# Weights laid out on the host so that each partition's row is contiguous: a recurrent attention and slot-memory layer on 8 cores

## The chip, the cores and the metric

The kernel runs as one program on all 8 cores of one Trainium2 chip. Each core owns 2048 of the 16384 token rows and writes that part of the output. Where a sum over the batch element is needed, a core goes through all 8192 rows of its batch element itself; the cores exchange nothing. The metric is the device time of the slowest core, in microseconds (us).

## What is computed

```python
x = L0_attn_q_x                      # (2, 8192, 1024)
xn = _layernorm(x)
s = attn(xn)                         # linear attention (elu + 1 features), wq, wk, wv, wo,
                                     # then an MLP 1024 -> 4096 -> 1024 (fc_w, proj_w)
g = silu(ffn(xn))                    # slot memory, below
return x + s * g

# ffn(x):
S = slot_init                        # 64 slots
ctx = concat(x, mean of S over the slots)
h = gelu(ctx @ w1 + b1)              # w1: (2048, 512)
route_logits = (h @ w2 + b2) / (abs(tau) + 0.1)
alpha = softmax over the top 8 of 64 logits
si = (alpha.T @ x) / alpha.sum(over rows)
S_new = GRU(si, S)                   # Wih, Whh: (3072, 1024)
q, k, v = S_new @ wq, S_new @ wk, S_new @ wv       # wq, wk: (1024, 256)
y = layernorm(S_new + softmax(q @ k.T * scale) @ v)
out = alpha @ (y @ wvp + bvp) @ wo + bo
```

The reference is in f32; the kernel multiplies in bf16 and holds sums in f32.

## The kernel before

`make_core_inputs` prepares each core's inputs on the host, `build_nc` writes the program. All weights come from HBM as f32 and are cast to bf16 on the way into SBUF, by DMAs that GpSimd (POOL) issues. The helper for this is `cast_load` (line 202): a weight of `nchunk` x 128 rows and `width` columns goes to an SBUF tile in which partition p holds row p of every chunk, side by side. Its source access pattern has three dimensions, so per partition it reads `nchunk` separate pieces of `width` f32 numbers:

```python
src = bass.AP(src_t.tensor, src_row0 * width,
              [[width, 128], [width * 128, nchunk], [1, width]])
```

The work is cut into blocks (`with nc.Block()`), and the engines meet in a barrier at the end of each block. Four blocks hold the loads that the change touches:

- Block 1 (line 309): SP issues 14 small loads of constants and then the first eight 512 KB tiles of x (`xld`). POOL issues w1ab (`w1a`, the upper half of w1: 8 chunks of 512 columns), w1bb (4 chunks of the lower half), w2b, slotTb, B2R, and eight tiny writes to `scr_qk`. Behind the barrier follow a few small operations on `tau` and the slot mean, and four matmuls on w1bb (line 379).
- Block 2 (line 390): POOL alone issues the other 4 chunks of w1bb, then wqb, wkb and wvb (8 chunks of 1024 columns each). Behind it come four matmuls on w1bb (line 405), a transpose and an addition, then phase A.
- Phase A (line 506): 16 tiles of 512 rows. For each: layernorm statistics (lines 524, 526), transposes, the multiplication with w1ab, logits, top 8, slot sums. wqb, wkb and wvb aren't used here; they are first read near 957 us.
- Block 3 (line 899): POOL issues a bias row, slotTb, fwqb and fwkb (8 chunks of 256 columns each) and four rows of whhT (1 chunk of 3072 columns each, 12 KB of f32 per partition). Behind it the slot GRU and the slot attention follow, with weights streamed in single chunks (whhT, wihT, fwv, wvp, fwo).
- Block 4 (line 1382): SP loads a mask; POOL issues wob (8 chunks of 1024 columns) and four bias rows. Behind it, attention and its output projection go through the 4 own tiles.

At the end the MLP runs. Its weights already lie on the host as 128 rows of 32768 numbers. fcw is loaded in pieces of 1024 numbers per partition (`load_fc`, line 1838) and pjw in pieces of 4096 (`load_pj`, 16 KB of f32 in one piece), both from rows 128 KB apart.

The DMAs increment semaphores (`swA` for w1, w2, fwq and fwk; `swB` for wq, wk, wv and wo), and `X` keeps the counts that later blocks wait for.

Of the kernel before, what the change touches and what calls it, by code (L numbers as in the profile page):

```python
# [14 lines left out]
D = 1024  # L15
# [6 lines left out]
NS, TOPK = 64, 8  # L22
DHF = 512
# [5 lines left out]
    return np.ascontiguousarray(np.asarray(v, np.float32).reshape(nchunk, 128).T)  # L29


def make_core_inputs(c, inp):
    import ml_dtypes
    BF = ml_dtypes.bfloat16
    g = lambda k: np.asarray(inp["L0_" + k], dtype=np.float32)
    b = c // 4
    r0 = (c % 4) * T_OWN
    x = g("attn_q_x")[b]
    return {
        "x8k": np.ascontiguousarray(np.concatenate([x[r0:], x[:r0]], axis=0)),  # L40
        "wq": g("attn_wq"), "wk": g("attn_wk"), "wv": g("attn_wv"),
        "wo": g("attn_wo"),
        "fcw": np.ascontiguousarray(
            g("attn_fc_w").reshape(8, 128, 4, 8, 128)
            .transpose(1, 2, 3, 0, 4).reshape(128, 32768)),
        "pjw": np.ascontiguousarray(
            g("attn_proj_w").reshape(32, 128, 8, 128)
            .transpose(1, 2, 0, 3).reshape(128, 32768)),
        "w1a": np.ascontiguousarray(g("ffn_w1")[0:D]),
        "w1b": np.ascontiguousarray(g("ffn_w1")[D:]),  # L50
        "w2": g("ffn_w2"),
        "wihT": np.ascontiguousarray(g("ffn_Wih").T),
        "whhT": np.ascontiguousarray(g("ffn_Whh").T),
        "fwq": g("ffn_wq"), "fwk": g("ffn_wk"), "fwv": g("ffn_wv"),
        "wvp": g("ffn_wvp"), "fwo": g("ffn_wo"),
        "slotT": np.ascontiguousarray(g("ffn_slot_init").T),
        "slot": g("ffn_slot_init"),
        "ln1w_c": _cols(g("attn_ln1_w"), 8), "ln1b_c": _cols(g("attn_ln1_b"), 8),
        "ln2w_c": _cols(g("attn_ln2_w"), 8), "ln2b_c": _cols(g("attn_ln2_b"), 8),
        "lng_c": _cols(g("ffn_ln_g"), 8), "lnb_c": _cols(g("ffn_ln_b"), 8),  # L60
        "fcb_c": _cols(g("attn_fc_b"), 32), "pjb_c": _cols(g("attn_proj_b"), 8),
        "b1_c": _cols(g("ffn_b1"), 4),
        "fbq_c": _cols(g("ffn_bq"), 2), "fbk_c": _cols(g("ffn_bk"), 2),
        "b2r": g("ffn_b2")[None, :],
        "bq_r": g("attn_bq")[None, :], "bk_r": g("attn_bk")[None, :],
        "bv_r": g("attn_bv")[None, :], "bo_r": g("attn_bo")[None, :],
        "bih_r": g("ffn_bih")[None, :], "bhh_r": g("ffn_bhh")[None, :],
        "fbv_r": g("ffn_bv")[None, :], "bvp_r": g("ffn_bvp")[None, :],
        "fbo_r": g("ffn_bo")[None, :],
        "tau": g("ffn_tau").reshape(1, 1),  # L70
        "identb": np.eye(128, dtype=np.float32).astype(BF),
        "identf": np.eye(128, dtype=np.float32),
        "mask4": np.ascontiguousarray(np.tile(
            (np.arange(128)[:, None] // 16 ==
             np.arange(128)[None, :] // 16).astype(np.float32), (1, 4))),
        "onesb": np.ones((1, 512), np.float32).astype(BF),
        "onecol": np.ones((128, 1), np.float32).astype(BF),
        "magic": np.full((128, 1), 0x5f3759df, np.int32),
        "zpad": np.zeros((1024, 64), dtype=BF),
    }  # L80


def build_nc(dbg=False):
    nc = bass.Bass("TRN2", target_bir_lowering=False)

    di = lambda n, s, dt=F32: nc.dram_tensor(n, s, dt, kind="ExternalInput").ap()
    x8k = di("x8k", [T_B, D])
    wq_d = di("wq", [D, D]); wk_d = di("wk", [D, D]); wv_d = di("wv", [D, D])
    wo_d = di("wo", [D, D])
    fcw_d = di("fcw", [128, 32768]); pjw_d = di("pjw", [128, 32768])  # L90
    w1a_d = di("w1a", [D, DHF]); w1b_d = di("w1b", [D, DHF]); w2_d = di("w2", [DHF, NS])
    wihT_d = di("wihT", [D, 3 * D]); whhT_d = di("whhT", [D, 3 * D])
    fwq_d = di("fwq", [D, 256]); fwk_d = di("fwk", [D, 256]); fwv_d = di("fwv", [D, D])
    wvp_d = di("wvp", [D, D]); fwo_d = di("fwo", [D, D])
    slot_d = di("slot", [NS, D]); slotT_d = di("slotT", [D, NS])
    ln1w_d = di("ln1w_c", [128, 8]); ln1b_d = di("ln1b_c", [128, 8])
# [39 lines left out]
    with ExitStack() as ex:  # L136
# [65 lines left out]
        def cast_load(g, dst2d, src_t, nchunk, width, dst_off=0, src_row0=0,  # L202
# [9 lines left out]
            else:  # L212
                C['wt'] += 16

        def chunked(t2d, nchunk, width):
            return t2d[:, 0:nchunk * width].rearrange("p (c w) -> p c w",
                                                      c=nchunk)
# [48 lines left out]
        with ExitStack() as exW:  # L266
# [6 lines left out]
            with ExitStack() as exA:  # L273
# [35 lines left out]
                with nc.Block() as blk:  # L309
                    @blk.sync  # L310
                    def _(s):
                        for src, dst in [(identb_d, cIDb[:]),
                                         (onesb_d, cONE[:]), (onecol_d, cCOL[:]),
                                         (magic_d, cMAG[:]),
                                         (b1_d, B1E[:]),
                                         (ln1w_d, LNC[:, 0:8]), (ln1b_d, LNC[:, 8:16]),
                                         (ln2w_d, LNC[:, 16:24]), (ln2b_d, LNC[:, 24:32]),
                                         (lng_d, LNC[:, 32:40]), (lnb_d, LNC[:, 40:48]),
                                         (fcb_d, BC[:, 0:32]), (pjb_d, BC[:, 32:40]),
                                         (fbq_d, FBC[:, 0:2]), (fbk_d, FBC[:, 2:4]),  # L320
                                         (tau_d, SCAL[0:1, 0:1])]:
                            dma(s, dst, src[:], sld, 'ld')
                        for st in range(4):
                            dmx(s, xslot(0, st), x8k[st * 128:(st + 1) * 128, :],
                                sx[0], 'x0')
                        for st in range(4):
                            r = 512 + st * 128
                            dmx(s, xslot(1, st), x8k[r:r + 128, :], sx[1], 'x1')

                    @blk.gpsimd  # L330
                    def _(g):
                        g.memset(SCAL[:, 7:8], EPS)
                        cast_load(g, w1ab, w1a_d, 8, DHF, sem=swA, key='wA')
                        cast_load(g, w1bb, w1b_d, 4, DHF, sem=swA, key='wA')
                        cast_load(g, w2b, w2_d, 4, NS, sem=swA, key='wA')
                        cast_load(g, slotTb, slotT_d, 8, NS, sem=swA, key='wA')
                        dmx(g, B2R[:], b2r_d[:], swA, 'wA')
                        for mt4 in range(4):
                            for half in range(2):
                                po = (mt4 * 8194 + half * 4097 + 4096) * 128  # L340
                                dmx(g, bass.AP(scr_qk, po, [[1, 128]]),
                                    bass.AP(zpad_d.tensor, 0, [[1, 128]]),
                                    swB, 'wB')
# [46 lines left out]
                with nc.Block() as blk:  # L390
                    @blk.gpsimd
                    def _(g):
                        cast_load(g, w1bb, w1b_d, 4, DHF, src_row0=512,
                                  sem=swA, key='wA')
                        cast_load(g, wqb, wq_d, 8, D, sem=swB, key='wB')
                        cast_load(g, wkb, wk_d, 8, D, sem=swB, key='wB')
                        cast_load(g, wvb, wv_d, 8, D, sem=swB, key='wB')

                with nc.Block() as blk:
                    @blk.tensor  # L400
# [466 lines left out]
            with ExitStack() as exB3:  # L867
# [31 lines left out]
                with nc.Block() as blk:  # L899
                    @blk.sync  # L900
                    def _(s):
                        dma(s, slotb[:], slot_d[:], sld, 'ld')

                    @blk.gpsimd
                    def _(g):
                        dmx(g, ROWB3[0:1, 0:3072], bhh_rd[:], swA, 'wA')
                        cast_load(g, slotTb2, slotT_d, 8, NS, sem=swA, key='wA')
                        cast_load(g, fwqb, fwq_d, 8, 256, sem=swA, key='wA')
                        cast_load(g, fwkb, fwk_d, 8, 256, sem=swA, key='wA')
                        for c0 in range(4):  # L910
                            cast_load(g, wslot(c0), whhT_d, 1, 3072,
                                      src_row0=c0 * 128,
                                      sem=swc4[c0], key=wk4[c0])
# [444 lines left out]
            with ExitStack() as exC:  # L1358
# [23 lines left out]
                with nc.Block() as blk:  # L1382
# [3 lines left out]

                    @blk.gpsimd
                    def _(g):
                        cast_load(g, wob, wo_d, 8, D, sem=swB, key='wB')
                        for srcd, i2 in [(bq_rd, 0), (bk_rd, 1), (bv_rd, 2),  # L1390
                                         (bo_rd, 3)]:
                            dmx(g, rowA(i2), srcd[:], swB, 'wB')
# [733 lines left out]
```

How the kernel before makes its waits and increments, by code:

```python
                    @blk.vector  # L348
                    def _(v):
                        v.wait_ge(sld, ld_p0)
                        v.wait_ge(swA, X['wA'])
                        t0 = SCAL[0:1, 0:1]
                        v.tensor_scalar(SCAL[0:1, 1:2], t0, -1.0, None, ALU.mult)
# [18 lines left out]
                    @blk.tensor  # L372
                    def _(t):
                        t.wait_ge(sdv, C['dv'])
                        t.matmul(pM0[:, 0:1], cONE[0:1, 0:128], SCB[0:1, 0:1],
                                 start=True, stop=True)
                        i = None
                        for cc in range(4):
                            i = t.matmul(pM1[0:1, 0:512], smT[:, cc:cc + 1],
                                         w1bb[:, cc * 512:(cc + 1) * 512],
                                         start=(cc == 0), stop=False)
                        fin(i, spe, 'pe')
# [1 line left out]
                    @blk.vector  # L384
                    def _(v):
                        v.wait_ge(spe, C['pe'])
                        i = v.tensor_copy(SCAL[:, 5:6], pM0[:, 0:1])
                        finv(v, sdv, 'dv')
# [11 lines left out]
                    @blk.tensor  # L400
                    def _(t):
                        t.wait_ge(swA, X['wA'])
                        i = None
                        for cc in range(4):
                            i = t.matmul(pM1[0:1, 0:512], smT[:, 4 + cc:5 + cc],
# [1441 lines left out]
                @blk.gpsimd  # L1847
                def _(g):
                    g.wait_ge(sy1, X['y1'])
                    for q in range(4):
```

## Time and profile before

| | us |
|---|---|
| median of 2 runs | 2354.45 (2351.16 to 2357.73) |
| profiled execution | 2343.93 |
| its span, slowest core (core 2) | 2342.4 |
| its span, fastest core (core 3) | 2321.8 |

| engine | busy us | share of the span |
|---|---|---|
| TensorE, matmul | 1206.5 | 52% |
| VectorE | 534.1 | 23% |
| ScalarE | 502.8 | 21% |
| GpSimd | 74.7 | 3% |

The profile is of core 2, the slowest. Times within it count from the first instruction of the core in question, so times of two cores are comparable only as far as the cores start together. "GB/s" in a row is what the DMA engines wrote: a weight that is read as f32 and written as bf16 counts with its bf16 bytes, and twice as many were read. The DMA share is the mean busy share of the core's 16 DMA engines; it goes over 1 where packets overlap. A packet is one contiguous piece of a DMA. The letter q behind an engine's name stands for its instruction queue: SPq and POOLq rows are DMA issues and waits, not work.

### The profile page before, as it was taken

Reading aid. Unit: us, or ns where it says so; the run is one execution under the profiler, and the core shown is the slowest. Engines: PE = TensorE matmul, PEld = TensorE weight load, DVE = VectorE, ACT = ScalarE, POOL = GpSimd, SP = SyncE. Lnnn points to the kernel's source line nnn. Section 1 sums busy time; section 2 is a strip of 40 time slices with the busy share of each in tenths; the row PEclk is TensorE's granted clock in tenths of the full one; section 3 lists DMA queues with packets and bytes.
Section 4 is the critical chain, followed back from the end, with each engine's and each line's share of the span. In section 5 each row is a group of like instructions: output and inputs, shape, how many; then the busy total and the mean of one; then the engine's idle time right before and its main releaser. Section 6 shows DMA issues by size and latency. Waiting matters only on the chain. (4 is left out here: it accounts for less than half of the span.)

```text
span 2342.4 us, 18749 instructions; the slowest of 8 cores (2321.8 to 2342.4 us)
## 1 busy us (share of the span) xinstructions
PE 1206.5 (52%) x6220; PEld 568.2 (24%) x6308; DVE 534.1 (23%) x1213; ACT 502.8 (21%) x748; POOL 74.7 (3%) x139
## 2 busy tenths in 40 slices
PE   0143535444533322644734825823078598598696
PEld 0021222222211100222321312311034243243242
DVE  0223133233210110323233233221210310400102
ACT  0144443443420100100100200200041330431521
POOL 1000000000000011000000000001100000000000
PEclk9976667777767555767867957957589799799798
DMA  7511011111046435152332331345903605506224
GB/s 133 107 52 72 36 72 37 71 72 71 2 59 120 73 51 85 50 104 63 86 68 63 86 77 54 99 77 119 196 14 72 180 1 101 151 11 120 85 39 105
DMA packets 185777, 183.65 MB, mean 78 GB/s; under 512 B 141331, under 2 KB 145556, under 8 KB 181588
## 3 DMA queue, kind: packets, MB, share of 16 engines
q0 software_dynamic: 26496, 72.72, 18.3%
q1 hardware_dynamic: 159188, 109.74, 16.3%
q8 instruction: 53, 0.87, 0.2%
q14 instruction: 40, 0.33, 0.0%
HBM read 204.81 MB, written 33.56 MB: 102 GB/s over the span
## 5 line engine op out<-in xcount | busy, mean ns | idle before, releaser
L690 PE MATMUL pM<-xnTs,w1ab 128*128 128x512 bf16 x496 | 141.9, 451 | 52.4 <-ACTq L199 52.0
L676 PE MATMUL pT<-cIDb,xnb 128*128 128x128 bf16 x256 | 31.6, 301 | 243.7 <-ACTq L199 156.2
L1948 DVE TENSOR_TENSOR y1t<-pTf,y1t 128x512 f32<-128x512 f32 x32 | 22.1, 692 | 503.0 <-PE pTf L2042 503.0
L2011 PE MATMUL pMa<-h2T,fcwb 128*128 128x512 bf16 x496 | 125.5, 393 | 21.2 <-ACTq L199 20.5
L2011 PE MATMUL pMb<-h2T,fcwb 128*128 128x512 bf16 x504 | 122.7, 386 | 0.4
L2028 PE MATMUL pPa<-g1F,pjcb 128*128 128x512 bf16 x500 | 111.8, 379 | 5.4 <-ACTq L199 4.5
L1611 ACT ACT_TABLE_LOAD x4 | 5.1, 1283 | 505.9 <-PE pBig L1564 505.9
L2028 PE MATMUL pPb<-g1F,pjcb 128*128 128x512 bf16 x504 | 112.7, 379 | 0.9 <-DMA pjcb<-pjw 0.2
L524 DVE BATCH_NORM_STATS2 ST<-xld 128x6 f32<-128x512 f32 x64 | 43.6, 681 | 281.6 <-ACTq L199 281.1
L1995 PE MATMUL pT0d<-cIDb,h2b 128*128 128x128 bf16 x128 | 16.3, 307 | 145.0 <-DVEq L199 84.5
L690 PEld LDWEIGHTS pM<-xnTs,w1ab 128*128 128x128 bf16 x512 | 56.0, 113 | 134.6 <-issue 99.5
L1440 PE MATMUL pBig<-wob,aoT 128*128 128x512 bf16 x248 | 71.0, 450 | 29.8 <-DVEq L199 29.8
L676 PEld LDWEIGHTS pT<-cIDb,xnb 128*128 128x128 bf16 x256 | 24.1, 135 | 250.6 <-issue 250.6
L1556 PE MATMUL pBig<-wqb,xhT 128*128 128x512 bf16 x252 | 64.3, 413 | 17.0 <-ACTq L199 16.1
L1777 DVE TENSOR_TENSOR AMK<-pBig,cMSK 128x512 bf16<-128x512 f32 x64 | 44.3, 692 | 121.6 <-PE pBig L1733 91.8
L2011 PEld LDWEIGHTS pMa<-h2T,fcwb 128*128 128x128 bf16 x512 | 50.9, 100 | 83.7 <-issue 27.7
L1733 PE MATMUL pBig<-FQ2h,FK2h 64*128 64x128 bf16 x256 | 31.2, 296 | 75.7 <-DMA scr_ao<-aog 69.5
L2011 PEld LDWEIGHTS pMb<-h2T,fcwb 128*128 128x128 bf16 x512 | 51.0, 100 | 63.8 <-issue 6.1
L2028 PEld LDWEIGHTS pPa<-g1F,pjcb 128*128 128x128 bf16 x512 | 49.6, 98 | 63.7 <-issue 6.8
L2070 ACT ACTIVATE h2T<-pT0d,LNC 128x128 bf16<-128x128 bf16 x128 | 58.5, 457 | 27.2 <-PE pT0d L1995 15.3
L2028 PEld LDWEIGHTS pPb<-g1F,pjcb 128*128 128x128 bf16 x512 | 49.8, 98 | 58.1 <-issue 1.3
L1752 PE MATMUL pBig<-V2h,AMK 128*128 128x64 bf16 x256 | 24.7, 214 | 73.1 <-DVEq L199 73.1
(263 smaller groups left out, 1721.0 us busy)
## 6 DMA issues: line engine op xcount, KB each, us to landing
xld<-x8k SPq DMA_DIRECT2D x64, 512.0 KB, 5.3
pjcb<-pjw POOLq DMA_DIRECT2D x32, 1024.0 KB, 8.7
scr_qk<-tmb SPq DMA_DIRECT2D x16, 512.0 KB, 2.6
y1scr<-XN SPq DMA_DIRECT2D x4, 2048.0 KB, 6.6
y1t<-y1scr SPq DMA_DIRECT2D x4, 2048.0 KB, 11.5
fcwb<-fcw POOLq DMA_DIRECT2D x32, 256.0 KB, 17.3
xre<-x8k SPq DMA_DIRECT2D x16, 512.0 KB, 10.1
out<-xre SPq DMA_DIRECT2D x16, 512.0 KB, 2.7
```

The costliest lines, as they stand in the source:

```text
L524: v.bn_stats(ST[:, SB[st]:SB[st] + 6], xslot(mt, st)[:, 0:512])
L676: i = t.transpose(dstb[:, cc * 128:(cc + 1) * 128], xb[:, cc * 128:(cc + 1) * 128], cIDb[:])
L690: i = t.matmul(dstp[:, 0:512], w1ab[:, cc * 512 + ch * 128: cc * 512 + (ch + 1) * 128], xnTs[:, cc * 512:(cc + 1) * 512], start=(cc == 0), ...
L1440: i = t.matmul(pBig0[:, nh * 512:(nh + 1) * 512], aoT[:, cc * 128:(cc + 1) * 128], wob[:, cc * 1024 + nh * 512: cc * 1024 + (nh + 1) * 512 ...
L1556: i = t.matmul(pBig0[:, nh * 512:(nh + 1) * 512], xhT[:, cc * 512 + st * 128: cc * 512 + (st + 1) * 128], wqb[:, cc * 1024 + nh * 512: cc ...
L1733: i = t.matmul(pBig0[:, (b % 2) * 512 + gl * 128: (b % 2) * 512 + (gl + 1) * 128], FK2h[0:64, g * 128:(g + 1) * 128], FQ2h[0:64, g * 128:( ...
L1752: t.matmul(pBig1[:, (B2 % 2) * 512 + gl * 64: (B2 % 2) * 512 + (gl + 1) * 64], amsl, V2h[:, g * 64:(g + 1) * 64], start=True, stop=True)
L1777: i = v.tensor_tensor(AMK[:, (b % 2) * 512:(b % 2 + 1) * 512], pBig0[:, (b % 2) * 512:(b % 2 + 1) * 512], cMSK[:], ALU.mult)
L1948: i = v.tensor_tensor(y1v(mt).rearrange("p (s w) -> p s w", s=4)[:, :, d * 128:(d + 1) * 128], pTf[:, :].rearrange("p (s w) -> p s w", s=4 ...
L2011: i = t.matmul(dstp[:, :], fcwb[:, m * 1024 + cc * 128: m * 1024 + (cc + 1) * 128], h2T[:, cc * 512:(cc + 1) * 512], start=(cc == 0), stop ...
L2028: i = t.matmul(dstp[:, :], pjcb[:, (d % 2) * 4096 + m * 128: (d % 2) * 4096 + (m + 1) * 128], g1F[:, m * 512:(m + 1) * 512], start=(m == 0 ...
L2070: i = a.activation(h2T[:, cc * 512 + st * 128: cc * 512 + (st + 1) * 128], pT0d[:, cc * 128:(cc + 1) * 128], AF.Identity, bias=LNC[:, 24 + ...
```

## The change

The host now stores eight weights (wq, wk, wv, wo, both halves of w1, and the slot attention's wq and wk) the way they will lie in SBUF: 128 rows, in row p the pieces of all chunks for partition p. A second helper, `cast_loadh`, reads them with two dimensions, one contiguous run per partition, into the same tile on the same semaphore. The lower half of w1 is loaded in two parts as before, columns 0 to 2047 and 2048 to 4095 of its row. Order, engines, semaphores and all other loads stay. w2, slotT, fwv, wvp, fwo, wihT and whhT keep their layout and `cast_load`.

```diff
+def _rm128(a):
+    n = a.shape[0] // 128
+    return np.ascontiguousarray(
+        a.reshape(n, 128, -1).transpose(1, 0, 2).reshape(128, -1))
...
-        "wq": g("attn_wq"), "wk": g("attn_wk"), "wv": g("attn_wv"),
-        "wo": g("attn_wo"),
+        "wq": _rm128(g("attn_wq")), "wk": _rm128(g("attn_wk")),
+        "wv": _rm128(g("attn_wv")),
+        "wo": _rm128(g("attn_wo")),
...
-        "w1a": np.ascontiguousarray(g("ffn_w1")[0:D]),
-        "w1b": np.ascontiguousarray(g("ffn_w1")[D:]),
+        "w1a": _rm128(g("ffn_w1")[0:D]),
+        "w1b": _rm128(g("ffn_w1")[D:]),
...
-        "fwq": g("ffn_wq"), "fwk": g("ffn_wk"), "fwv": g("ffn_wv"),
+        "fwq": _rm128(g("ffn_wq")), "fwk": _rm128(g("ffn_wk")),
+        "fwv": g("ffn_wv"),
...
+        def cast_loadh(g, dst2d, src_t, nchunk, width, col0=0, tot=None,
+                       sem=None, key=None):
+            tot = nchunk * width if tot is None else tot
+            src = bass.AP(src_t.tensor, col0, [[tot, 128], [1, nchunk * width]])
+            g.dma_start(out=dst2d[:, 0:nchunk * width],
+                        in_=src).then_inc(sem, 16)
+            X[key] += 16
...
-                        cast_load(g, w1ab, w1a_d, 8, DHF, sem=swA, key='wA')
-                        cast_load(g, w1bb, w1b_d, 4, DHF, sem=swA, key='wA')
+                        cast_loadh(g, w1ab, w1a_d, 8, DHF, sem=swA, key='wA')
+                        cast_loadh(g, w1bb, w1b_d, 4, DHF, tot=4096,
+                                   sem=swA, key='wA')
...
-                        cast_load(g, w1bb, w1b_d, 4, DHF, src_row0=512,
-                                  sem=swA, key='wA')
-                        cast_load(g, wqb, wq_d, 8, D, sem=swB, key='wB')
-                        cast_load(g, wkb, wk_d, 8, D, sem=swB, key='wB')
-                        cast_load(g, wvb, wv_d, 8, D, sem=swB, key='wB')
+                        cast_loadh(g, w1bb, w1b_d, 4, DHF, col0=2048,
+                                   tot=4096, sem=swA, key='wA')
+                        cast_loadh(g, wqb, wq_d, 8, D, sem=swB, key='wB')
+                        cast_loadh(g, wkb, wk_d, 8, D, sem=swB, key='wB')
+                        cast_loadh(g, wvb, wv_d, 8, D, sem=swB, key='wB')
...
-                        cast_load(g, fwqb, fwq_d, 8, 256, sem=swA, key='wA')
-                        cast_load(g, fwkb, fwk_d, 8, 256, sem=swA, key='wA')
+                        cast_loadh(g, fwqb, fwq_d, 8, 256, sem=swA, key='wA')
+                        cast_loadh(g, fwkb, fwk_d, 8, 256, sem=swA, key='wA')
...
-                        cast_load(g, wob, wo_d, 8, D, sem=swB, key='wB')
+                        cast_loadh(g, wob, wo_d, 8, D, sem=swB, key='wB')
```

## Rows read from the trace of the kernel before

**Rows 1.** The page: its head, and the queue of POOL's DMAs.

```profile
span 2342.4 us, 18749 instructions; the slowest of 8 cores (2321.8 to 2342.4 us)
...
q0 software_dynamic: 26496, 72.72, 18.3%
```

**Rows 2.** Operations at the four lines (ns min/median/max, first and last start us).

```profile
L309 POOLq DRAIN  x1: 30830/30830/30830, 6.9 to 6.9; - x1
...
L390 POOLq DRAIN  x1: 44234/44234/44234, 45.0 to 45.0; - x1
...
L899 POOLq DRAIN  x1: 27932/27932/27932, 682.6 to 682.6; - x1
...
L1382 POOLq DRAIN  x1: 13783/13783/13783, 923.7 to 923.7; - x1
```

**Rows 3.** Timeline, 0 to 140 us: start us, us, instruction.

```profile
1.60 1.04 POOL L208 DMA_DIRECT2D w1ab<-w1a  x1 [0.44 <-issue]
...
14.07 100.35 SPq L191 DMA_DIRECT2D xld<-x8k  x12
...
43.68 0.81 POOL L208 DMA_DIRECT2D w1bb<-w1b  x1 [34.29 <-PEq L390]
...
89.65 1.86 PE L405 MATMUL pM<-w1bb,smT 128*1 128x512 bf16 x4 [47.08 <-PEq L390]
```

**Rows 4.** DMA: an issue (KB, median us to landing); all packets of 40 to 95 us.

```profile
B2R<-b2r POOLq DMA_DIRECT2D x1, 0.1 KB, 30.1
...
DMA packets 3648, 6.82 MB, mean 124 GB/s; under 512 B 64, under 2 KB 576, under 8 KB 3648
```

**Rows 5.** Stretches, core 2: busy us by engine, PEclk, DMA share, GB/s.

```profile
4.00:8.00 4.00, 0.00 (x0) 0.00 (x0) 0.00 (x0) 0.00 (x0) 4.00 (x9) 1.00 0.95 92
8.00:14.00 6.00, 0.00 (x0) 0.00 (x0) 0.00 (x0) 0.00 (x0) 1.39 (x3) 1.00 1.12 136
46.00:47.00 1.00, 0.00 (x0) 0.00 (x0) 0.00 (x0) 0.00 (x0) 1.00 (x2) 1.00 0.04 3
48.00:88.00 40.00, 0.00 (x0) 0.00 (x0) 0.00 (x0) 0.00 (x0) 0.00 (x0) 1.00 1.07 168
684.00:692.00 8.00, 0.00 (x0) 0.00 (x0) 0.00 (x0) 0.00 (x0) 0.92 (x2) 0.50 1.18 148
692.00:700.00 8.00, 0.00 (x0) 0.00 (x0) 0.00 (x0) 0.00 (x0) 0.00 (x0) 0.50 1.02 159
700.00:704.00 4.00, 0.00 (x0) 0.00 (x0) 0.00 (x0) 0.00 (x0) 0.00 (x0) 0.50 1.02 209
924.00:932.00 8.00, 0.00 (x0) 0.00 (x0) 0.00 (x0) 0.00 (x0) 0.85 (x2) 0.50 1.08 193
1642.00:1654.00 12.00, 0.00 (x0) 0.00 (x0) 0.00 (x0) 0.00 (x0) 3.09 (x7) 0.50 1.07 158
1837.00:1839.00 2.00, 2.00 (x11) 0.89 (x10) 0.00 (x0) 0.00 (x0) 0.00 (x0) 1.00 1.11 233
1845.00:1849.00 4.00, 2.12 (x4) 0.39 (x4) 2.45 (x2) 2.16 (x5) 0.00 (x0) 0.61 1.04 178
2306.00:2307.00 1.00, 0.03 (x1) 0.06 (x1) 0.00 (x0) 0.69 (x1) 0.53 (x1) 1.00 0.00 0
```

**Rows 6.** The same view for core 3.

```profile
692.00:700.00 8.00, 0.00 (x0) 0.00 (x0) 0.00 (x0) 0.00 (x0) 0.00 (x0) 0.50 0.95 146
700.00:704.00 4.00, 1.82 (x5) 0.85 (x6) 0.00 (x0) 0.00 (x0) 0.00 (x0) 0.50 0.01 2
```

**Rows 7.** The same view: first core 0, then core 1.

```profile
43.00:48.00 5.00, 0.00 (x0) 0.00 (x0) 0.00 (x0) 0.00 (x0) 0.00 (x0) 1.00 1.15 206
...
43.00:46.00 3.00, 0.00 (x0) 0.00 (x0) 0.00 (x0) 0.00 (x0) 3.00 (x4) 1.00 0.05 4
```

**Rows 8.** Timeline of POOL: two DMA issues.

```profile
922.01 0.91 POOL L208 DMA_DIRECT2D wob<-wo  x1 [9.13 <-PEq L1382]
...
2306.39 0.53 POOL L1868 DMA_DIRECT2D pjcb<-pjw  x1 [8.12 <-PE pPb L2028]
```

More of the change, by code:

```diff
@@ L87, in build_nc @@
     x8k = di("x8k", [T_B, D])
-    wq_d = di("wq", [D, D]); wk_d = di("wk", [D, D]); wv_d = di("wv", [D, D])
-    wo_d = di("wo", [D, D])
+    wq_d = di("wq", [128, 8192]); wk_d = di("wk", [128, 8192])
+    wv_d = di("wv", [128, 8192]); wo_d = di("wo", [128, 8192])
     fcw_d = di("fcw", [128, 32768]); pjw_d = di("pjw", [128, 32768])
-    w1a_d = di("w1a", [D, DHF]); w1b_d = di("w1b", [D, DHF]); w2_d = di("w2", [DHF, NS])
+    w1a_d = di("w1a", [128, 4096]); w1b_d = di("w1b", [128, 4096])
+    w2_d = di("w2", [DHF, NS])
     wihT_d = di("wihT", [D, 3 * D]); whhT_d = di("whhT", [D, 3 * D])
-    fwq_d = di("fwq", [D, 256]); fwk_d = di("fwk", [D, 256]); fwv_d = di("fwv", [D, D])
+    fwq_d = di("fwq", [128, 2048]); fwk_d = di("fwk", [128, 2048])
+    fwv_d = di("fwv", [D, D])
     wvp_d = di("wvp", [D, D]); fwo_d = di("fwo", [D, D])
```

## The prediction

> **What bounds the kernel now.** I read first the page's head and its DMA queues. The span is 2342.4 us on the slowest core and 2321.8 us on the fastest, and the queue of POOL's DMAs, the one that all the edited loads use, is busy for only 18.3% of it [rows 1]. So most of the span (TensorE, ScalarE and VectorE working in a chain) can't be touched by a layout of weights. Next I read the operations recorded at the lines of the four blocks in which the edited loads stand. Each of these blocks ends in a barrier, and before it POOL runs a DRAIN that lasts until POOL's own DMAs have landed: 30.8, 44.2, 27.9 and 13.8 us, 116.7 us together [rows 2]. I call the blocks 1 to 4. No compute engine works in that time. The timeline shows it: the first of the four loads of block 2, w1bb, is issued at 43.68, and the matmul at line 405, which needs nothing but this w1bb (0.52 MB, first in the queue), starts at 89.65 [rows 3]. What the barrier waits for is the last, wvb, which the kernel first multiplies much later. So a microsecond taken from one of these four drains is a microsecond of the span, and this holds for nothing else in the change.
>
> The question is therefore what sets the speed of these loads: the number of pieces, or the bytes. In the stretch of block 2 the trace counts 3648 packets for 6.82 MB [rows 4]. That is one per row piece of 4 KB f32 (3 x 1024, 2 KB when written as bf16) or 2 KB f32 (512), and 64 small ones. The rate is 168 GB/s written, so 336 GB/s read, at a DMA share of 1.07: the engines always have something to do [rows 5].
>
> **The pairs.** In block 3 whhT arrives in rows of 12 KB f32, 6 KB written, three times larger than the pieces of wq. Core 2 gets 159 GB/s there from 692 to 700 us. At 700 core 3 falls from 146 to 2 GB/s, and core 2 rises to 209 [rows 5, 6]. So two neighbouring cores share something, and what a core gets depends on the other one. Held against this, the small pieces do as well: core 0 loads its second w1bb and the beginning of wq (1 KB and 2 KB written) at 206 GB/s between 43 and 48 us, while core 1 moves 4 GB/s [rows 7]. With the neighbour at work, pieces of 2 KB get 168 (wq, wk, wv) and 158 (fcw, rows 128 KB apart), pieces of 6 KB 159 and pieces of 8 KB (pjw) 178. Alone, 2 KB gets 193 to 206, 6 KB 209, 8 KB 233 [rows 5, 7]. Under load, which is how all cores stand in blocks 1 and 2, there is no gain in the size of the piece.
>
> **The change part by part.** It touches w1 (1.57 MB written in block 1, 0.52 MB in block 2), wq, wk and wv (6.29 MB, block 2), fwq and fwk (1.05 MB, block 3) and wo (2.10 MB, block 4), 11.54 MB in all. Bytes, order, semaphores, barriers and what lands where in SBUF stay as they are. Each load becomes 128 rows instead of 512 or 1024 pieces, so the queue's 26496 packets [rows 1] fall by 896 (w1a), 2 x 384 (w1b), 4 x 896 and 2 x 896, to 19456. The edited loads now take about 11.6 us (1.57 MB at 136 GB/s, block 1), 40.6 us (6.82 at 168), 7.1 us (1.05 at 148) and 10.9 us (2.10 at 193) [rows 5], together 70 us.
>
> Block 2. First the start. w1bb is issued at 43.68 and its data flows from about 47.0 (3 GB/s in the microsecond before) [rows 3, 5]: 3.3 us for 512 pieces, with 3072 more behind them. A load of 128 pieces, pjcb at 2306.39, moves data from 2307 on (0 GB/s before) [rows 5, 8]: 0.6 us. The difference, 2.7 us, is the upper bound. The lower is 0, for part of those 3.3 us may be paid by any first DMA after a barrier. I take 2.0, nearer to the pjcb row. Then the rate: 168 stays, 0 us. The lower bound is the slowest loaded row, 158, which costs 6.82/0.158 - 40.6 = +2.6 us. The upper is 209, worth -8.0 us. I take the row of pieces three and four times larger under load (159, 178), which brackets what is there.
>
> The Trainium skill has a price for a small packet (DMA: Bandwidth & Descriptors, "Why small descriptors are slow"): about 3 cycles on top of one per 32 bytes. As an estimate from that page, this would make 1 KB pieces 9% and 2 KB pieces 4 to 5% faster once they are long, some 4.5 us over all edited loads, and a result near 2344. The 206 GB/s of pieces of 1 and 2 KB beside 209 of 6 KB don't show it.
>
> Block 1. w1ab is issued at 1.60 and 92 GB/s flow between 4 and 8 us; from 8 to 14 us, before x is asked for, it is 136 [rows 3, 5]. At the 168 of block 2 the 1.57 MB would take 9.4 us instead of 11.6: 2.2 us, and data after 0.6 instead of 2.4 us adds up to 1.8. But what the drain waits for is not w1: the tiny B2R, issued before the drain begins at 6.9 us, needs 30.1 us to land [rows 2, 4], while the eight x loads (4.2 MB, issued by SP from 14.07 us [rows 3]) run on the same engines until the drain ends at 37.7. What the weights free must first be used by x. Bounds 0 and 4.0; I take 2.0.
>
> Block 3. slotT stays in 1024 small pieces in front. fwq and fwk, with the smallest pieces of all edited loads (512 bytes written), come between 684 and 692 us, at 148 GB/s [rows 5]: 7.1 us. At 168 they would take 6.2, so 0.9 us is the gain in rate, and up to 1 more if POOL's making of 2048 descriptors holds up whhT behind them; nothing at least. I take 1.0.
>
> Block 4. wob is issued at 922.01 and the drain ends at 923.7 + 13.8 = 937.5 [rows 2, 8]: 15.5 us, of which 10.9 are data at 193 GB/s. The rest is the start, four bias rows and the end. The start can give back 2.7 us at most, as in block 2, and nothing at least; a mask load of SP fills part of it, so I take 1.0.
>
> The rest costs nothing: POOL's issues get shorter, but POOL goes straight into its drain. The weights are used long after, so no later wait changes, and a stall doesn't move to another place: the barrier is released by the same DMA a little earlier. Should w1 become faster than x in block 1, x is late next, and that is the 0 of its bound.
>
> **Sum.** 2.0 + 2.0 + 1.0 + 1.0 = 6.0 us. The profiled execution took 2343.9 us (span 2342.4 and 1.5 around it), so it would be 2337.9. The median shown is 2354.45, 10.5 above it, and its two runs lie 6.6 us apart. From the median I come to 2354.45 - 6.0 = 2348.
>
> **The rivals.** A, the layout doesn't bring larger packets: if the rows are cut again into the old pieces, all stays, 2354.5. For it: each row of 32 KB f32 is longer than any piece of before (16 KB f32, pjw). Against: the pieces that the code asks of POOL with pjw's uncut (24064), and 16 small packets for each of its 134 DMAs as in block 2 (64 for 4), come to 26208, close to the 26496 counted [rows 1, 4].
>
> B, the pieces do set the rate under load. Then what is shared by a pair would serve long rows better, and all edited bytes come at 209 GB/s: 11.54/0.209 = 55 instead of 70 us, and with 4 us of starts the gain is 19: 2335. For it: 8 KB alone does best (233). Against: 159 and 178 under load, beside 168 for the pieces of now.
>
> C, the long rows are slower. Pieces that were neighbours in one 512 KB stretch of HBM become 128 streams whose starts lie 32 KB apart (16 KB for w1, 8 KB for fwq), and such streams may hit the same part of the memory. If all edited loads fell to the poorest rate of a busy stretch, 92 GB/s (4 to 8 us) [rows 5], they would take 11.54/0.092 = 125 us, 55 more: 2409, slower by 2.3%. It decides against the change once the edited loads together take more than the 4 us that the starts give back, at a mean of 11.54/74 = 156 GB/s against 11.54/70 = 165 now, and it passes 2% (47 us) at 99 GB/s. Against it: fcw and pjw already have rows 128 KB apart and get 158 and 178 under load [rows 5]. The Trainium skill has such a rule (DMA: Bandwidth & Descriptors, "Latency and other measured facts"): row pitches of large powers of two slow a copy, halving it at 4 MiB. The pitches here are far below those it lists, and no run here shows it.
>
> **How the numbers follow.** The small gain of the sum 0.62, A 0.16, B 0.10, C in a mild form (up to +20 us) 0.08, C in full 0.04. The range runs from under B's 2335 to a mild C or a poor run, 2328 to 2362; the two runs of before alone span 2351 to 2358. Faster by over 2% (about what a measurement of this kernel can tell from no change, 47 us) would need 40% of all four drains: 0.01. Slower by over 2% is C in full: 0.04. Within 2%: 0.95.
>
> **What the profile after would show.** The queue of POOL at about 19456 packets; 576 packets for 6.82 MB in block 2; issues of the edited loads at the 0.53 us of pjcb [rows 8] instead of 0.9; the DRAIN of line 390 ending near 85 us instead of 45.0 + 44.2 = 89.2 [rows 2] (2.0 from block 1 and 2.0 of its own; its start moves with the shorter issues, so its end is what counts), and the one of 1382 about a microsecond shorter; the rate of block 2 near 168. If that rate is 200 or more, B is right and I have taken a limit of pieces for one of the pair. If it is under 150, C is. If all this holds and the time still moves by more than 10 us, the cause lies outside these blocks, for instance in the rhythm of the long phases (the cores of before already differ by 20 us [rows 1]), and my sum was of the wrong thing.

## The result, and the profile after

| | before | after |
|---|---|---|
| median, us | 2351.85 (10 runs) | 2335.68 (12 runs) |
| ratio, after to before | | 0.9922, 95% interval 0.9901 to 0.9943 |
| profiled execution, us | 2343.93 | 2330.59 |
| span, slowest core | 2342.4 | 2329.0 |
| span, mean of the 8 cores | 2333.1 | 2320.4 |

The change takes 0.8%, some 16 to 18 us, where 6 had been forecast: inside the range, faster, and nearly three times the gain. The mean span fell by 12.7 us, the profiled execution by 13.3. The ratios, unlike the medians, leave out every execution in which one half of the cores ran at a lower granted clock, and where the profiled execution was such a one (w1 of block 1 alone, below), its drains are means over the other four cores.

First the page of the changed kernel, its head and the queue of POOL's DMAs (packets, MB, share of the 16 engines). Behind it, all packets of the stretch from 40 to 95 us on core 2 of a kernel described below ("all but that"), whose block 2 has the changed loads and nothing beside them:

```profile
span 2329.0 us, 18837 instructions; the slowest of 8 cores (2307.1 to 2329.0 us)
...
q0 software_dynamic: 19456, 72.72, 18.6%
```

```profile
DMA packets 576, 6.82 MB, mean 124 GB/s; under 512 B 64, under 2 KB 64, under 8 KB 192
```

The packets are those foretold, 19456 and 576, so the rows arrive whole, and rival A is out. The engines' share of the queue, though, is 18.6% against 18.3% [rows 1] for the same bytes (core 2 in both kernels: 18.1 and 18.3): with a quarter fewer packets the DMA engines are busy for about as long.

The four drains of the slowest core, core 7 (operations at the four lines: ns min/median/max, first and last start us), which answer to [rows 2]:

```profile
L327 POOLq DRAIN  x1: 17590/17590/17590, 6.9 to 6.9; - x1
...
L409 POOLq DRAIN  x1: 44918/44918/44918, 31.7 to 31.7; - x1
...
L918 POOLq DRAIN  x1: 28779/28779/28779, 668.5 to 668.5; - x1
...
L1401 POOLq DRAIN  x1: 15102/15102/15102, 909.4 to 909.4; - x1
```

The slowest core isn't the same in both profiles, and cores differ, so the comparison goes by the mean of all eight:

| mean over the cores, us | block 1 | block 2 | block 3 | block 4 | sum |
|---|---|---|---|---|---|
| drain, before | 30.2 | 42.6 | 28.3 | 14.1 | 115.2 |
| drain, after | 16.7 | 44.3 | 27.6 | 12.7 | 101.4 |
| end of the drain, before | 37.1 | 86.9 | 706.6 | 931.6 | |
| end of the drain, after | 23.6 | 75.2 | 695.1 | 920.7 | |

Nearly everything comes from block 1: 13.5 us, of which block 2 takes 1.8 back. The 11 to 12 us that are left after block 2 stay, but for a fraction: 10.9 at the end of block 4's drain.

The same core in both kernels shows where it happens. DMA issues of core 2 up to 39 us (KB, us from issue to landing), first before, then after:

```profile
w1ab<-w1a POOLq DMA_DIRECT2D x1, 1024.0 KB, 13.3
...
slotTb<-slotT POOLq DMA_DIRECT2D x1, 128.0 KB, 18.1
```

```profile
w1ab<-w1a POOLq DMA_DIRECT2D x1, 1024.0 KB, 10.2
...
slotTb<-slotT POOLq DMA_DIRECT2D x1, 128.0 KB, 12.8
...
B2R<-b2r POOLq DMA_DIRECT2D x1, 0.1 KB, 13.2
```

w1ab, the largest load whose layout changed here, lands only 3.1 us sooner. slotTb, which didn't change, gains 5.3 us, and the 128 bytes of B2R gain 17: 13.2 instead of 30.1 [rows 4]. Most of the gain is at loads that the change doesn't touch.

Stretches of the changed kernel on core 2 (columns as in [rows 5]):

```profile
4.00:8.00 4.00, 0.00 (x0) 0.00 (x0) 0.00 (x0) 0.00 (x0) 4.00 (x9) 1.00 0.98 166
8.00:14.00 6.00, 0.00 (x0) 0.00 (x0) 0.00 (x0) 0.00 (x0) 0.81 (x2) 1.00 1.10 152
...
24.00:32.00 8.00, 1.26 (x3) 0.13 (x1) 0.16 (x1) 0.00 (x0) 2.19 (x4) 1.00 1.03 319
...
48.00:72.00 24.00, 0.00 (x0) 0.00 (x0) 0.00 (x0) 0.00 (x0) 0.00 (x0) 1.00 1.00 170
```

At the start w1 flows faster (166 and 152 GB/s against 92 and 136). From 48 to 72 us, when wq, wk and wv come in their long rows, it is 170 against 168 [rows 5]: nothing. And between 24 and 32 us x still flows (319 GB/s, nearly all of it x), while the drain of block 1 has been over since 20.4 us and the first matmuls run. POOL's drain no longer lasts as long as x does.

### The profile page after: what moved, and what is told of

Read it like the earlier page. It is cut to its first block and busy times, and to the rows that moved or that the text cites. A ratio compares the mean times of both kernels' runs of the same rounds, so it can differ in the third digit from the quotient of the medians.

```text
span 2329.0 us, 18837 instructions; the slowest of 8 cores (2307.1 to 2329.0 us)
## 1 busy us (share of the span) xinstructions
PE 1215.7 (52%) x6308; PEld 567.2 (24%) x6308; DVE 533.7 (23%) x1213; ACT 503.0 (22%) x748; POOL 71.8 (3%) x139
## 3 DMA queue, kind: packets, MB, share of 16 engines
q0 software_dynamic: 19456, 72.72, 18.6%
q1 hardware_dynamic: 159188, 109.74, 16.7%
## 5 line engine op out<-in xcount | busy, mean ns | idle before, releaser
L709 PE MATMUL pM<-xnTs,w1ab 128*128 128x512 bf16 x512 | 149.2, 459 | 44.5 <-ACTq L209 44.2
L543 DVE BATCH_NORM_STATS2 ST<-xld 128x6 f32<-128x512 f32 x64 | 43.6, 681 | 280.6 <-ACTq L209 280.0
L2030 PEld LDWEIGHTS pMa<-h2T,fcwb 128*128 128x128 bf16 x512 | 50.8, 100 | 84.3 <-issue 28.3
L2089 ACT ACTIVATE h2T<-pT0d,LNC 128x128 bf16<-128x128 bf16 x128 | 58.6, 458 | 27.3 <-PE pT0d L2014 15.3
```

The lines of the kernel that those rows point to most:

```text
L543: v.bn_stats(ST[:, SB[st]:SB[st] + 6], xslot(mt, st)[:, 0:512])
L709: i = t.matmul(dstp[:, 0:512], w1ab[:, cc * 512 + ch * 128: cc * 512 + (ch + 1) * 128], xnTs[:, cc * 512:(cc + 1) * 512], start=(cc == 0), ...
L2030: i = t.matmul(dstp[:, :], fcwb[:, m * 1024 + cc * 128: m * 1024 + (cc + 1) * 128], h2T[:, cc * 512:(cc + 1) * 512], start=(cc == 0), stop ...
L2089: i = a.activation(h2T[:, cc * 512 + st * 128: cc * 512 + (st + 1) * 128], pT0d[:, cc * 128:(cc + 1) * 128], AF.Identity, bias=LNC[:, 24 + ...
```

## The experiments

The drains are means over the cores of one profiled execution each, in us. Ratios are to the kernel before on the same chip, with 95% intervals. Not all kernels ran on the same chip, so they are compared with each other through their ratios.

| kernel | block 1 | block 2 | block 3 | block 4 | ratio |
|---|---|---|---|---|---|
| before | 30.2 | 42.6 | 28.3 | 14.1 | |
| after | 16.7 | 44.3 | 27.6 | 12.7 | 0.9922 (0.9901 to 0.9943) |
| w1 of block 1 alone (cores 4 to 7) | 17.0 | 45.7 | 29.7 | 14.9 | 0.9956 (0.9939 to 0.9973) |
| all but that | 28.7 | 42.7 | 27.2 | 12.8 | 0.9973 (0.9947 to 1.0000) |
| before, x held back | 15.6 | 46.6 | 29.7 | 15.9 | 0.9978 (0.9958 to 0.9999) |
| after, x held back | 14.0 | 46.4 | 28.6 | 12.4 | 0.9945 (0.9925 to 0.9965) |
| after, x first | 26.5 | 43.6 | 28.4 | 12.9 | one execution, no ratio |
| before, small loads first | 31.1 | 43.8 | 29.3 | 15.2 | 1.0016 (0.9982 to 1.0051) |
| after, w2 and slotT in rows too | 15.3 | 44.1 | 27.3 | 12.6 | 0.9924 (0.9895 to 0.9954) |
| after, wq, wk, wv at the start of phase A | 16.2 | 9.8 | 28.3 | 12.6 | 0.9792 (0.9756 to 0.9829) |
| the last two together | 15.5 | 8.5 | 26.2 | 13.0 | 0.9811 (0.9767 to 0.9855) |
| after, wq, wk, wv spread over phase A | 15.5 | 9.6 | 28.8 | 13.4 | 0.9776 (0.9736 to 0.9815) |
| before, wq, wk, wv spread over phase A | 30.4 | 6.3 | 29.6 | 15.1 | 0.9856 (0.9823 to 0.9888) |

The drain of block 1 before is 31.4 us over cores 4 to 7 alone, 30.2 over all eight.

**The change in two parts.** First block 1's loads of w1 alone:

```diff
-                        cast_load(g, w1ab, w1a_d, 8, DHF, sem=swA, key='wA')
-                        cast_load(g, w1bb, w1b_d, 4, DHF, sem=swA, key='wA')
+                        cast_loadh(g, w1ab, w1a_d, 8, DHF, sem=swA, key='wA')
+                        cast_loadh(g, w1bb, w1c_d, 4, DHF, sem=swA, key='wA')
```

> The kernel before, with only the two loads of w1 in block 1 changed (one contiguous row per partition). Turns theory: each DMA engine takes packets by turns from POOL's queue and SP's, so the small packets behind w1 in POOL's queue (w2b, slotTb, B2R) wait for the x packets of SP once those flow; w1 in fewer packets lets them out before. Then this edit alone shortens the drain of block 1 from a mean of 30.2 us over the cores to about 17 (16.7 in the changed kernel), and gives 11 to 14 of the 16 us: about 2339. Rate theory (long rows are served faster everywhere, my rival B): the gain goes with the bytes, 1.57 of 11.54 MB, so about 2 to 3 us here: about 2349.

Then everything but these two loads:

> The changed kernel, with the two loads of w1 in block 1 put back to pieces: wq, wk, wv, wo, fwq, fwk and the second part of w1b stay contiguous. Turns theory: the drain of block 1 stays at 30 us; block 2 gains its start of 1 to 2 us, block 3 0 to 1, block 4 1.4, in all 3 to 5 us: about 2348. Rate theory: 12 to 14 of the 16 us: about 2338, and the drain of block 2 falls from 42.6 to 36 or less.

w1 alone makes the drain short, 31.4 to 17.0 us as expected, and gives 0.44%, 10 us, a little less than the 11 to 14 expected. All the rest, 9.97 of 11.54 MB, gives 0.27%, 6 us, and leaves block 1 at 28.7. Together that is 0.71% of the 0.78. The intervals of the two ratios overlap (6 to 14 us and 0 to 12), so the times alone don't say which part gives more. But 14% of the bytes bring 10 us, where rival B, by bytes, leaves them 2 to 3, and the drains show where the gain is. So rival B falls although the time of 2335 was its own. The second kernel also gives the clean price of the layout in block 2, since no x runs beside it there, as in the kernel before. Core 2, drain and stretch:

```profile
L409 POOLq DRAIN  x1: 42721/42721/42721, 43.3 to 43.3; - x1
...
48.00:84.00 36.00, 0.00 (x0) 0.00 (x0) 0.00 (x0) 0.00 (x0) 0.00 (x0) 1.00 1.00 162
```

162 GB/s in rows of 16 KB written, 168 in pieces of 2 KB [rows 5], and a mean drain of 42.7 against 42.6 us. A load under way with the neighbour working gains nothing from longer pieces here. The drains of blocks 3 and 4 got 1.1 and 1.3 us shorter. Over all rows of the table block 4's drain is 14.1 to 15.9 us with the old layout of wo and 12.4 to 13.4 with the new, so that about 2 us there are real; in block 3 the two groups overlap (28.3 to 29.7, and 26.2 to 28.8).

**x held back.** SP waits until w1ab, w1bb, w2b, slotTb and B2R have landed (5 x 16) before it asks for x; in the first kernel no layout is changed:

```diff
+                        s.wait_ge(swA, 80)
                         for st in range(4):
                             dmx(s, xslot(0, st), x8k[st * 128:(st + 1) * 128, :],
                                 sx[0], 'x0')
```

> The kernel before, layout untouched; SP asks for x only when w1ab, w1bb, w2b, slotTb and B2R have landed. Turns theory: without x packets to take turns with, the drain of block 1 falls from 30.2 to about 15 us (w1bb landed at 17.7 us, and slotTb and B2R follow in 3 to 5 us), with no layout changed; x then loads beside block 2, whose drain grows by up to 8 us, so the time falls by 5 to 12 us: 2340 to 2347. Descriptor theory (POOL's making of 3584 descriptors holds B2R up, whatever SP does): the drain stays at 26 us or more, and as x comes later the time doesn't fall.

> The changed kernel with the same wait of SP before x. Turns theory: the drain of block 1 is 9 to 13 us on all cores alike (it was 13.5 to 23.1 without the wait), and against the run of the kernel before with this wait the layout is worth only 2 to 4 us in this drain. Time 2332 to 2338, about as the changed kernel. Descriptor theory: a difference of 12 us or more between the two kernels with the wait, as without it.

The drain of block 1 on core 2, in pieces with x held back:

```profile
L309 POOLq DRAIN  x1: 15819/15819/15819, 6.9 to 6.9; - x1
```

Half of the 30.8 us of before [rows 2] are gone with the old layout, and on all cores alike (14.9 to 16.2, where it was 26.1 to 34.8). So the number of pieces in itself, or POOL's making of their descriptors, doesn't hold this drain up: x does. The layout is worth 1.6 us of drain once x is out of the way (15.6 to 14.0); 2 to 4 had been expected, and 9 to 13 us for the drain of 14.0. The time moves less than the drain: 0.9978, 5 us, at the edge of the 5 to 12 expected. x comes later, and in block 2 the drain grows by 4.0 us because x now runs beside it. In the changed kernel the wait gives nothing (0.9945 and 0.9922, the intervals overlap). Block 2 also begins later after the drain, for SP is still issuing x: its drain ends at 78.9, 8.0 us sooner than before. In the kernel in pieces even that is gone by the end of block 4's drain (931.0 against 931.6), with phase A, block 3 and block 4 a little longer each; why is not settled.

**x first.** The changed kernel, with SP's eight x loads ahead of its small ones (the list in the code has 16 of these, not the 14 named ahead of the prediction):

> The changed kernel with the eight x loads issued by SP ahead of its 14 small loads, so that x flows from the start instead of from 11 to 15 us on. Turns theory: now the small packets of POOL's queue (96 per DMA engine for w2b and slotTb) meet the 64 x packets per engine in spite of the contiguous w1, and the drain of block 1 grows from a mean of 16.7 back to 24 us or more, where x ends. If the layout of w1 in itself made the drain short, it stays near 17.

The drain of block 1 and two of the landings on core 2:

```profile
L327 POOLq DRAIN  x1: 26513/26513/26513, 6.9 to 6.9; - x1
...
w1ab<-w1a POOLq DMA_DIRECT2D x1, 1024.0 KB, 14.4
...
slotTb<-slotT POOLq DMA_DIRECT2D x1, 128.0 KB, 25.2
```

With contiguous w1 the drain is long again, 26.5 us in the mean, once x flows from the start. w1ab, first in POOL's queue with 8 large packets per DMA engine, has landed 14.4 us after its issue. slotTb, an eighth of its bytes in 64 small packets per engine, takes 25.2; it stands behind w1ab, w1bb and w2b in the same queue, so this time isn't the price of its own packets alone. What happens in between is seen in the packets of the two queues, q1 of SP (x and the constants) and q0 of POOL (packets, MB, share of 16 engines), on core 2, first from 20 to 26 us, then from 26 to 30:

```profile
q1 hardware_dynamic: 515, 1.79, 86.5%
q0 software_dynamic: 516, 0.06, 16.3%
...
q1 hardware_dynamic: 1914, 0.30, 80.0%
q0 software_dynamic: 1299, 0.13, 53.3%
```

Beside x, POOL's queue gets 516 packets of 128 bytes out in 6 us, one for one of SP's, although it moves a thirtieth of the bytes. From 26 us on, as x runs out (its last packet is through at 28.4), 1299 go in 4 us. The other seven cores show the same, 488 to 559 packets of POOL's beside 495 to 560 of SP's from 20 to 26 us.

**Small loads first.** The kernel before, only POOL's order in block 1 changed; w1ab and w1bb come last:

```diff
-                        cast_load(g, w1ab, w1a_d, 8, DHF, sem=swA, key='wA')
-                        cast_load(g, w1bb, w1b_d, 4, DHF, sem=swA, key='wA')
                         cast_load(g, w2b, w2_d, 4, NS, sem=swA, key='wA')
...
                                     swB, 'wB')
+                        cast_load(g, w1ab, w1a_d, 8, DHF, sem=swA, key='wA')
+                        cast_load(g, w1bb, w1b_d, 4, DHF, sem=swA, key='wA')
```

> The kernel before with only the order of POOL's issues in block 1 changed: w2b, slotTb, B2R and the writes to scr_qk ahead of w1ab and w1bb; the layout stays in pieces, the packet counts too. Turns theory: the 96 tiny packets per engine go out before x flows and 96 packets of 1 KB meet x instead; the drain ends once those have had their turns, somewhere between 17 and 25 us long instead of 30.2, and the time falls by 3 to 10 us. If the number of packets in POOL's queue against the 64 of x per engine is all that counts, the order changes nothing: 28 us or more, as half of the 1 KB packets are still there at 14 us.

```profile
w1ab<-w1a POOLq DMA_DIRECT2D x1, 1024.0 KB, 25.3
...
slotTb<-slotT POOLq DMA_DIRECT2D x1, 128.0 KB, 3.5
```

My 17 to 25 us were wrong, the other figure held: 31.1 us. slotTb now lands after 3.5 us instead of 18.1, but w1ab, in 64 pieces per engine, needs 25.3 instead of 13.3 in the old order. The order chooses the victim, and here too the queues go one for one: 815 packets each on core 2 from 20 to 34 us, POOL's of 1 KB, SP's mostly of 4 KB. The order moved more than I had reckoned with. w1ab is issued at 7.75 us instead of 1.60, behind the eight writes to `scr_qk`, and SP, through with its small loads earlier, asks for x at 8.30 instead of 14.07. So nearly all of w1 met x, where I had expected half of it to be out. Whether an order that gets part of w1 out first would gain anything, no run shows. What decides is how many packets POOL's queue still has when x begins, and they can be pieces of w1 as well as of slotT.

**Fewer pieces still.** w2 and slotT stored in rows as well:

> The changed kernel with w2 and slotT stored as contiguous rows as well (256 packets in place of 1536 in block 1, 128 in place of 1024 in block 3). Turns theory: w2b and slotTb need 8 packets per engine instead of 32 and 64, everything of POOL's is through before x packets matter, and the drain of block 1 falls from a mean of 16.7 to 11 to 13 us on all cores alike; block 3 gives 1 to 3 us more. About 6 us less than the changed kernel: near 2331, ratio 0.989 to 0.992. If pieces don't matter beyond w1: no difference to the changed kernel.

15.3 instead of 16.7 us in block 1, and no gain that can be told from the changed kernel (0.9924 and 0.9922). I had expected 11 to 13, and 1 to 3 us in block 3, where 27.3 against 27.6 shows nothing. With x held back and w2b and slotTb in pieces it is 14.0 as well, so something near 14 us is a floor that neither x nor the pieces of w2 and slotT set. The packets' times in the kernel after with x held back say what fills it, in means over the cores: the last packet of w1 is through at 15.3 us, the last of POOL's queue at 17.8, and the drain, begun at 6.9, ends at 20.9. So 8.4 of its 14.0 us are w1 itself. The last 3.0 us, without packets, are only 0.5 in block 2 and 0.9 where w1 comes last (small loads first); the writes to `scr_qk`, last in this queue otherwise, may be the reason, which no run tried apart. Nor were SP's small loads, which run beside w1.

**What the barrier needn't wait for.** wq, wk and wv are moved out of block 2 into phase A, first all at its start:

> The changed kernel with the loads of wq, wk and wv issued in the block of phase A instead of block 2, so that no barrier waits for them. If the drain of block 2 is on the path microsecond for microsecond, it falls from 44 to 6 to 10 us and the time by 35 us to near 2300 (ratio about 0.978); phase A hides 6.3 MB. If those loads rather delay the x tiles of phase A by as much, the first tiles take longer and less than half of it is left.

> Both of the last two edits together: the sum of their gains, about 2294 (ratio about 0.975). Should their gains overlap (the drain of block 1 hides behind the x loads that phase A waits for once block 2 is short), it is no faster than the one with wq, wk and wv moved alone.

The drain of block 2 falls to 9.8 us and ends at 38.8 us instead of 75.2, 36 us sooner, and the ratio is 0.9792, near the 0.978 expected. But the end of the drain in block 3 moves by 27 us only (695.1 to 667.9). VectorE's waits in the first of the two kernels, core 3, 40 to 700 us (us in total, times, longest):

```profile
DVE ST L546 <- ACTq L209: 257.8, 14, 24.8
...
DVE ST L546 <- DMA xld<-x8k: 31.4, 1, 31.4
```

Once it waits 31.4 us for x instead of up to 25 for ScalarE: the weights and the third set of x tiles share the DMA engines. With w2 and slotT in rows too there is no further gain (0.9811, the intervals overlap). So each load is issued behind a tile of its own:

```diff
+                    @blk.gpsimd
+                    def _(g):
+                        g.wait_ge(sdv, v_apply(4, 3))
+                        cast_loadh(g, wqb, wq_d, 8, D, sem=swB, key='wB')
+                        g.wait_ge(sdv, v_apply(7, 3))
+                        cast_loadh(g, wkb, wk_d, 8, D, sem=swB, key='wB')
+                        g.wait_ge(sdv, v_apply(10, 3))
+                        cast_loadh(g, wvb, wv_d, 8, D, sem=swB, key='wB')
```

> The changed kernel with wq, wk and wv loaded inside phase A, one after each of the tiles 4, 7 and 10, instead of all at its start. With all at its start the third set of x tiles was late (VectorE idle for 31.4 us on xld at 94 us), and 9 of 36 us saved in block 2 were given back. If that collision is the whole loss, the end of the drain in block 3 falls from 668 to about 659 us and the time to near 2297 (ratio about 0.975). If phase A pays for 6.3 MB wherever they come, it stays near 0.979.

> The kernel before (pieces everywhere) with the same three loads inside phase A. It asks whether the layout is still worth something once block 2 is short: then phase A starts when x has landed (near 36 to 40 us in both kernels) rather than when POOL's drains end. Turns theory with x as the next to be late: block 1 still costs 30 us but block 2 only about 7 after it, since nothing of x is left; drain of block 2 ends near 50 against 39, so some 11 us of the layout's gain stay: ratio about 0.980 to 0.982. If x hides it: same ratio as the changed kernel with these loads moved.

The wait for x is gone from the list on cores 2 and 5, and the drain of block 3 ends at 659.6 (659 expected). The ratio, 0.9776, is the lowest of all (0.975 expected), but its interval overlaps that of 0.9792. With the old layout the same move gives 0.9856. The layout's 0.8% is there again, because the next to be late is still POOL: block 1's drain ends at 37.3 in pieces and 22.4 in rows, 14.9 us apart, and block 2's at 49.5 and 37.9, 11.6 apart, for in rows x now runs beside it (9.6 us against 6.3). I had left the layout 11 us and put the ratio at 0.980 to 0.982; the gap is right, the kernel is slower than I said.

## Why the prediction was right and wrong

- **Where the time lies: right in the main.** What the four drains gave (13.8 us in sum) is near what the spans lost (12.7 in the mean). In between it isn't microsecond for microsecond: by the end of block 4's drain 10.9 us are left, and 1.8 come behind it. The 16 to 18 us of the medians and the ratio are a little more; one profiled execution can't settle those few us.
- **The time: inside the range, in part by luck.** 2348 was forecast. The 2335.68 measured lies near the lower end of 2328 to 2362, which reached so far down only for rival B, whose mechanism isn't there. The last sign named, that a move of more than 10 us would mean a cause outside the four blocks, was wrong: the drain of line 390 ends at 73.8 us on core 2, not near 85, and the cause lies in block 1.
- **The packets: right,** 19456 and 576.
- **Rate under load: right.** 0 us in block 2 was the term, and 162 to 170 GB/s against 168 were measured. The old layout gives 161 to 168 there (161 in the kernel with w1 alone). What bounds it is told with the pairs in the prediction, and no run here spoke against it. Two of its readings were wrong without harm: the slowest loaded row is 146 GB/s (core 3, 692 to 700 us [rows 6]), not 158, and the 233 for pieces of 8 KB weren't reached alone, for core 3 moves 162 GB/s in the same 2 us of its own time.
- **Start of block 2, 2.0 us: wrong, 0.** 42.7 against 42.6 us. It is the lower bound that I had written down and not taken. The 3.3 us were those of core 2, and I hadn't read the others: in the kernel before, POOL's first packet flows 1.5 to 1.7 us after the issue on five of the eight cores and 2.9 to 3.2 on three, with rows (all but w1 of block 1) 1.3 us on five and 2.3 to 2.5 on three. So most of the 3.3 us isn't the price of 512 pieces, and the few tenths that rows start sooner don't show in the drain.
- **Blocks 3 and 4, 1.0 each: right within what one execution tells,** 0.6 and 1.4 us (1.1 and 1.3 in the kernel without w1 of block 1; nearer 2 in block 4 by all rows of the table).
- **Block 1, 2.0 us with bounds 0 and 4.0: wrong by far, 13.5.** This is the term that failed, and its upper bound was no bound. The arithmetic of the step was sound for w1: it lands 3 us sooner. The conclusion was not. I read B2R landing late, next to the end of x, and wrote that what the weights free must first be used by x. I took x as work that has to be finished anyway. But no one waits for x there: SP's own drain at line 309 took 0.12 us on core 2, and x may flow on into block 2, as it does from 24 to 32 us in the changed kernel. I never asked why 128 bytes take 30 us.
- **What takes its place.** Data packets of POOL's queue per DMA engine: in pieces 64 + 32 + 32 + 64 = 192 (w1ab, w1bb, w2b, slotTb), in rows 8 + 8 + 32 + 64 = 112; x has 64. The engines serve the two queues packet by packet in turn, so each packet of POOL's that is left when x begins waits for one of x's 4 KB, and if more than 64 are left on an engine, the queue isn't through before x is. Three runs bear this out from three sides. Without x the drain is short in pieces too (15.6). With x first it is long in rows too (26.5). With the small loads first the pieces of w1 wait instead (31.1).
- **The packets show it directly:** 516 beside 515, 815 beside 815, and in the kernel before itself 793 of POOL's beside 785 of SP's (core 4, 20 to 30 us). So does what is left when x begins (its sixteenth packet), completions counted: 827 to 1710 of POOL's 3424 packets in the kernel before, 0 to 127 of 2144 on seven cores of the changed one. The eighth, core 0, has 691 left, and its drain is the longest, 23.1 us. The rows count by stretches of all 16 engines; the order on a single engine they don't show. The Trainium skill says in "Queues, rings and completion order" of DMA: Bandwidth & Descriptors that each engine goes round the queues it has work for at packet granularity. The trace agrees, in the packets that the profile counts, with the 516 beside 515. The prediction used another section of that page: by "Why small descriptors are slow" in the Trainium skill, pieces of 1 and 2 KB should have cost some 4.5 us over all edited loads, as an estimate, and 42.7 against 42.6 us doesn't show it.
- **Rival B gave the right time for the wrong reason.** Its mechanism (209 GB/s under load) is refuted by 162 to 170. **Rival C** isn't there either: with rows 32 KB apart the rate is 162 to 170 GB/s and the drain of block 2 the same. (Its 99 GB/s for 2% leave out the 4 us of starts that the sentence before counts; with them it is 95.)

## What to carry to other kernels

Before weighing how fast a load becomes, ask what its barrier waits for and what that last thing stands behind: here it was a few small loads at the end of one queue with many small packets, beside another queue full of large ones. There it pays to cut the number of packets in that queue; holding the bulk back shortened the drain as much and gave less time (0.2%). The bytes per second don't show any of it. And a drain that waits for weights which nobody reads for 870 us is worth more than any layout: moved behind the tiles of the next phase, those loads gave 35 us of drain, over twice what the change gave.

## What the runs showed of the hardware that was not expected

- A DRAIN of POOL waits for POOL's DMAs (15.1 to 44.9 us on core 7 of the changed kernel), while x, which SP issued, flows on beyond the barrier, at 319 GB/s on core 2 from 24 to 32 us.
- Two queues share the DMA engines by packets, not by bytes: from 20 to 26 us of the kernel with x first, 516 packets of 128 bytes went out beside 515 of the other queue, mostly of 4 KB (0.06 MB beside 1.79).
- How soon a POOL load begins after its issue differs between the cores of one execution: 1.5 to 3.2 us in block 2 of the kernel before.
- Rows of 32 KB f32, written as 16 KB, count as one packet each (576 for 6.82 MB, 384 of them such rows) and bring no rate under load (162 GB/s against 168).
